# A slot list built from one-hot factors: token columns laid out in pairs, the 112-column factor held stationary

## The reference

```
topv, topi = lax.top_k(probs, K)                          # K = 2 experts for each token
mask = flat_i[None, :] == jnp.arange(E)[:, None]
pv, pp = lax.top_k(jnp.where(mask, flat_v[None, :], -1.0), capacity)
tok = jnp.where(pv > 0.0, pp // K, 0)
xin = x_flat[tok]                                         # 8 x 444 rows of 256
h = gelu(einsum('ecd,edh->ech', xin, w1) + b1)
out_e = (einsum('ech,eho->eco', h, w2) + b2) * w
out = zeros.at[tok.reshape(-1)].add(out_e)                # then a layer norm and the residual
```

## Time and profile before

| | |
|---|---|
| median of 3 runs | 497.82 us (497.4 to 695.03) |
| profiled execution | 497.69 us, its span 496.0 us |
| mean granted TensorE clock | 0.861 of 2.4 GHz |
| busy: PE, DVE, ACT, POOL | 376.4, 330.7, 210.0, 239.3 us |

### The profile page before, as it was taken

The page is one execution under the profiler, slowest core; times in us unless marked ns, Lnnn a source line. Parts: engine busy times, 40 slices in busy tenths (PEclk is TensorE's granted clock), DMA queues, the critical chain, the costliest instruction groups (busy, mean ns, idle before and its releaser), DMA issues.

```text
span 496.0 us, 7921 instructions
## 1 busy us (share of the span) xinstructions
PE 376.4 (76%) x2309; PEld 333.4 (67%) x2309; DVE 330.7 (67%) x863; ACT 210.0 (42%) x466; POOL 239.3 (48%) x399
## 2 busy tenths in 40 slices
PE   4585999999999998430136799999999999992000
PEld 1485999999999997330023599999999999991000
DVE  6463688777787866788881366667666676740692
ACT  4222445445445443272000256565656556532241
POOL 3254777777777755300002600835537274044395
PEclk9779899999999998755555699999999999997555
DMA  6423123323323201290002323656546475132833
GB/s 188 108 85 104 45 76 103 91 74 109 86 78 109 65 28 58 74 152 1 0 22 83 92 86 106 150 156 165 114 130 138 151 173 134 17 39 28 212 92 105
DMA packets 44676, 47.42 MB, mean 96 GB/s; under 512 B 11851, under 2 KB 36550, under 8 KB 44646
## 3 DMA queue, kind: packets, MB, share of 16 engines
q1 hardware_dynamic: 37940, 38.91, 28.0%
q0 software_dynamic: 5632, 7.36, 9.1%
q10 hardware_dynamic: 1074, 0.79, 0.6%
HBM read 32.38 MB, written 14.67 MB: 95 GB/s over the span
## 4 chain that ended last, share of the span: by engine, by line
PE 69%; DVE 12%; POOL 6%; DMA 4%; SPq 3%; issue 2%; ACT 1%; ACTq 0%; POOLq 0%; DVEq 0%
PE pz L796 16%; PE pall L809 16%; PE pall L703 9%; PE pall L672 8%; DVE wproj L1071 5%; PE pall L679 3%; SPq L423 3%; PE pall L769 2%; PE pall L713 2%; PE pz L659 2%; POOL stage L1354 2%; PE pall L720 1%; PE pall L821 1%; DMA stage<-in_x 1%; PE pall L692 1%
## 5 line engine op out<-in xcount | busy, mean ns | idle before, releaser
L1325 POOL DMA_INDIRECT y_rows<-rows,didx x32 | 50.7, 1585 | 95.2 <-ACT rows L606 87.9
L796 PE MATMUL pz<-halves 128*128 128x448 f32 x384 | 90.6, 373 | 2.1 <-DVE halves L1153 2.1
L809 PE MATMUL pall<-halves 128*128 128x448 f32 x384 | 89.9, 369 | 0.6 <-DVE halves L1148 0.6
L796 PEld LDWEIGHTS pz<-halves 128*128 128x128 f32 x384 | 73.7, 192 | 8.8 <-DVE halves L1153 2.5
L809 PEld LDWEIGHTS pall<-halves 128*128 128x128 f32 x384 | 70.9, 188 | 6.8 <-DVE halves L1148 1.0
L590 ACT ACTIVATE wproj<-pz,b1t 128x448 f32<-128x448 f32 x64 | 40.6, 635 | 73.8 <-PE pz L796 70.3
L1315 POOL DMA_INDIRECT rows<-x_rows,gidx x32 | 34.6, 1082 | 69.6 <-DVE gidx L1133 60.0
L703 PE MATMUL pall<-halves 128*112 128x256 f32 x396 | 55.1, 296 | 9.0 <-DVE halves L981 9.0
L1146 DVE CAST halves<-wproj 128x448 fp32r<-128x448 f32 x64 | 26.6, 416 | 50.0 <-ACT wproj L590 46.0
L703 PEld LDWEIGHTS pall<-halves 128*112 128x112 f32 x396 | 50.8, 186 | 9.9 <-DVE halves L981 7.4
L1223 POOL TENSOR_TENSOR rs<-rs,neghalf 112x1 f32<-112x1 f32 x88 | 50.1, 570 | 7.3
(11 more groups left out here) (211 smaller groups left out, 736.3 us busy)
## 6 DMA issues: line engine op xcount, KB each, us to landing
stage<-in_w SPq DMA_DIRECT2D x32, 512.0 KB, 4.2
stage<-in_x SPq DMA_DIRECT2D x64, 108.0 KB
x_rows<-x SPq DMA_DIRECT2D x22, 224.0 KB, 3.3
y_rows<-zero SPq DMA_DIRECT2D x22, 112.0 KB
stage<-y_rows SPq DMA_DIRECT2D x3, 448.0 KB, 5.4
out<-stage SPq DMA_DIRECT2D x7, 192.0 KB
scratch<-y_rows SPq DMA_DIRECT2D x2, 448.0 KB, 8.5
wproj<-in_w_proj ACTq DMA_DIRECT2D x1, 768.0 KB
```

What stands on the lines that cost most here:

```text
L796: m = nc.tensor.matmul(bank(k % 2)[:, 0:SLOTS], w[:, c, k * 128:(k + 1) * 128], xs[:, e % 2, c, :], start=(n == 0), stop=(n == 3 * EC - 1))
L809: m = nc.tensor.matmul(pall[:, 2 * (e % 2) + o, 0:SLOTS], w[:, k, o * 128:(o + 1) * 128], hs[:, k % 2, :], start=(k == 0 and n == 0), stop ...
L1325: pool.indirect_dma_start(y_rows, bass.IndirectOffsetOnAxis(ap=didx[:, k:k + 1], axis=0), y[:, e % 2, j, :], None, compute_op=ALU.add).the ...
```

## The change

The two factors get another layout, the matmul's operands change places, and the transposition behind it goes.

- `ohlo` is laid out as [22 pairs, 112 rows, 2] and `ohhi` and `ohval` as [22 pairs, 32 columns, 2]: the innermost two elements are the token columns 2i and 2i+1. Neighbouring columns of one q are then 2 elements, 4 bytes, apart.
- The tables hold each number twice in place of 44 times, and the comparisons read them again for each pair (`each_pair`), as they read `hi`, `lo` and `code` again for each column (`by_pair`). The number of elements that each DVE instruction computes stays the same: 1408, 1408, 2464 and 2464.
- Each of the 44 matmuls takes `ohlo` (112 columns) as the stationary operand and `ohval` (32 columns) as the moving one. The result is [112, 32], in the bank from which `gidx` was read before.
- The copy to `listT`, the transpose, and the two waits between them are gone.

```diff
-        ohlo = rows[:, 0:Q * P // 2].bitcast(bf16).rearrange("p (c q) -> p c q", q=Q)
-        ohhi = rows[:, Q * P // 2:Q * (P + COLS) // 2].bitcast(bf16).rearrange("p (c q) -> p c q", q=Q)
+        ohlo = rows[:, 0:Q * P // 2].bitcast(bf16).rearrange("p (q c k) -> p q c k", c=P, k=2)
+        ohhi = rows[:, Q * P // 2:Q * (P + COLS) // 2].bitcast(bf16).rearrange("p (q c k) -> p q c k", c=COLS, k=2)
-        ohval = sb("ohval", [P, COLS, Q], bf16)
+        ohval = sb("ohval", [P, Q // 2, COLS, 2], bf16)
-        lotab = sb("lotab", [P, P, Q], bf16)
-        hitab = sb("hitab", [P, COLS, Q], bf16)
-        listT = sb("listT", [COLS, P])
+        lotab = sb("lotab", [P, P, 2], bf16)
+        hitab = sb("hitab", [P, COLS, 2], bf16)
-        def over_q(a):
-            return rep(a.rearrange("p (a q) -> p a q", a=1), 1, COLS)
+        def by_pair(a, n):
+            return rep(a.rearrange("p (q a k) -> p q a k", a=1, k=2), 2, n)
+
+        def each_pair(tab, n):
+            return rep(tab.rearrange("p (a c) k -> p a c k", a=1), 1, n)
-            nc.scalar.copy(hitab[:, :, :], rep(iorow[:, 0:COLS].rearrange("p (c a) -> p c a", a=1), 2, Q)).then_inc(r_tab, 1)
-            nc.scalar.copy(lotab[:, :, :], rep(locen[:, :].rearrange("p (c a) -> p c a", a=1), 2, Q)).then_inc(r_tab, 1)
+            nc.scalar.copy(hitab[:, :, :], rep(iorow[:, 0:COLS].rearrange("p (c a) -> p c a", a=1), 2, 2)).then_inc(r_tab, 1)
+            nc.scalar.copy(lotab[:, :, :], rep(locen[:, :].rearrange("p (c a) -> p c a", a=1), 2, 2)).then_inc(r_tab, 1)
-                m = nc.tensor.matmul(bank(6)[0:COLS, 0:P], ohval[:, :, q], ohlo[:, :, q],
+                m = nc.tensor.matmul(bank(7)[0:P, 0:COLS], ohlo[:, q // 2, :, q % 2], ohval[:, q // 2, :, q % 2],
                                      start=(q == 0), stop=(q == Q - 1))
             m.then_inc(r_list, 1)
-            pe.wait_ge(r_list, 2)
-            nc.tensor.transpose(bank(7)[0:P, 0:COLS], listT[:, :], ident[0:COLS, 0:COLS]).then_inc(r_list, 1)
-            link(V_.tensor_tensor(ohhi, over_q(hi[:, :]), hitab[:, :, :], ALU.is_equal))
-            V_.tensor_tensor(ohval[:, :, :], ohhi, over_q(code[:, :]), ALU.mult).then_inc(r_val, 1)
+            link(V_.tensor_tensor(ohhi, by_pair(hi[:, :], COLS), each_pair(hitab[:, :, :], Q // 2), ALU.is_equal))
+            V_.tensor_tensor(ohval[:, :, :, :], ohhi, by_pair(code[:, :], COLS), ALU.mult).then_inc(r_val, 1)
             link(V_.scalar_tensor_tensor(lo[:, :], hib[:, :], -float(P), s12f, ALU.mult, ALU.add))
             for h in range(2):
-                qs = slice(h * Q // 2, (h + 1) * Q // 2)
-                V_.tensor_tensor(ohlo[:, :, qs], rep(lo[:, qs].rearrange("p (a q) -> p a q", a=1), 1, P),
-                                 lotab[:, :, qs], ALU.is_equal).then_inc(r_lo, 1)
+                qs = slice(h * Q // 4, (h + 1) * Q // 4)
+                V_.tensor_tensor(ohlo[:, qs, :, :], by_pair(lo[:, h * Q // 2:(h + 1) * Q // 2], P),
+                                 each_pair(lotab[:, :, :], Q // 4), ALU.is_equal).then_inc(r_lo, 1)
             dve.wait_ge(r_list, 1)
-            V_.tensor_copy(listT[:, :], bank(6)[0:COLS, 0:P]).then_inc(r_list, 1)
-            dve.wait_ge(r_list, 3)
-
             listed = bank(7)[0:P, 0:COLS].bitcast(u32)
```

## The result

The changed kernel takes 490.07 us in the median of 4 runs (489.28 to 490.32), the kernel before 497.61 (495.08 to 695.03): a ratio of 0.9846 with a 95% interval of 0.9824 to 0.9868. In a second comparison on one chip with three other kernels it was 489.28 against 497.41, 0.9825 (0.980 to 0.985). Forecast were 489.9 us and a range of 488.4 to 494.0. The 695.03 us is one slow run among the four of before, and the ratio leaves it out.

The account below looks back on a forecast made before the run. The prediction took the single file of routing work, with 44 list matmuls at 88 bytes between columns, as the bound: 497.69 - 7.95 (`gidx` earlier) + 0.1 (clock) = 489.8 us, stated as 489.9, range 488.4 to 494.0.

Parts of the forecast that it names:

- The spacing of the matmuls: List matmuls on TensorE: 0.094 us from start to start in place of 0.260, the price of a 112-column load.
- the rival that rested on the other reading, 188 ns a pair: List matmuls: the stationary operand is read at the rate of 4-byte data, 493.9 us; chance 0.10.
- the one with 260: List matmuls: any gap between columns costs what it does now, leaving the transposition's 0.65 us, 497.0 us; chance 0.04.
- The sum: List stage: matmuls at 0.094 us, copy and transpose gone; `gidx` moves from 268.10 to 260.15, 7.95 us.
- The list's length: The 44 list matmuls: first at 255.82 as now, last start 259.86, list done at 260.12.
- The comparisons: DVE's comparisons before the list keep their counts and times, 0.89 and 1.44 us.
- the slower rival: DVE comparisons: each row of two elements costs extra; at 5.2 ns a row, 509 us; chance 0.03.
- The collision with the weights: Gathers behind `gidx`: the first two meet the second expert's weights, the last does not; charged nothing, up to 1 us as bound.
- The margin to the splits: Before `gidx`: DVE's splits end at 259.42 and do not hold it; margin 0.7 us.
- The clock: TensorE at the feed-forward start: same cold start, no gain from the shorter list; 0.1 us added, bound 2.3 less or more.
- the 4 to 5 given as a sign: Feed-forward start: if the forecast is right, the clock rises 4 to 5 us behind the first L796.
- the case better than the sum: Loads shorter, `gidx` follows the splits at 259.45, clock rises 1 us or more earlier: below 487.9 us; chance 0.03.

Follow-up runs that it names:

- three other kernels: Changed kernel plus unread matmuls: 18 behind the list, 487.87 us; 20 more in front, 488.71; the same with index ahead of the w2 splits, 488.37.
- the runs on the pitch: Changed kernel with 1, 4, 11 or 22 token columns side by side instead of 2 (2, 8, 22, 44 bytes): 492.67, 490.20, 493.82, 494.20 us.
- the run with 2 bytes: Changed kernel with the columns of one token column side by side, no pairs, each row of the comparisons one token column: 492.67 us.
- The last run above: Changed kernel plus 18 unread matmuls behind the list and 20 in front, with the index ahead of the two w2 splits on DVE: 488.37 us, 0.9812.
- the repeat: The changed kernel itself run again, on one chip with three kernels given extra matmuls: 489.28 us, 0.9825 against before.
- the two profiles whose list began at 2.4 GHz: Changed kernel with unread matmuls on both sides of the list, 488.71 us, and the same with index ahead of the w2 splits, 488.37 us.

## Why the prediction was right, point by point

- **The spacing of the matmuls.** Predicted 0.094 us from the difference of two loads, measured 0.093. This is the term that carries the forecast, and the runs on the pitch bear it out: 112 close columns cost 112 cycles, in either place. The guess that a contiguous f32 load goes over its columns twice was not tested by itself, but the rival that rested on the other reading, 188 ns a pair, is refuted, and so is the one with 260.
- **Pitch, not operand.** The sum charged the load's 112 columns as it would have charged 112 moving ones. The run with the old operand order shows that this was sound at 4 bytes (0.093 us apart at 1.2 GHz in either place), and that the swap is the small part. At 88 bytes the two differ: 0.214 and 0.260.
- **The list's length.** Predicted 4.30 us from the first matmul's start to the end (255.82 to 260.12), measured 4.27; `gidx` 4.33 behind the start, measured 4.29. The step at `gidx` was 7.95, measured 7.99.
- **The comparisons.** Taken as unchanged, and unchanged. The Trainium skill (Vector Engine (DVE) Microarchitecture Reference, section 5.1) has two results a cycle for 16-bit operands with step one and an innermost count above one; the trace agrees at a count of 2 (0.89 us for 1408), and the run with 2 bytes shows the lost rate (1.63) once an operand is read at step 0. A cost for each row of two, the slower rival, is below what the trace resolves.
- **The collision with the weights.** It is there, as forecast, and hidden, as forecast. The first gathered block is transposed 3.63 us behind its issue (259.88 to 263.51) where it was 3.05, but the last lands 2.65 us behind its issue against 2.70. The last run above has a stronger collision: the second gather landed 4.52 us after its issue, still ahead of the last, and it cost 0.6 us through what had queued up behind it on TensorE, filling matmuls among it.
- **The margin to the splits.** 0.7 us predicted, 0.68 measured as DVE's wait.
- **The clock.** No rise inside the list and a cold start of the same kind: right. The rise itself came 3.5 us behind the first L796 in the first profile and 5.3 in the repeat, both outside the 4 to 5 given as a sign (and before it was 4.4; 4.7 was the end of the window that the prediction read). Mis-sized was the price of the cold start. Its bound of 2.3 us up or down took all of the half-clock stretch as time on the path; the runs show 1.1 to 1.7 in all, because ACT and DVE take 1.9 us behind the first 6 matmuls whatever the clock, and the next 6 have that time to run in. A rise 1 us earlier, on which the case better than the sum counted, is worth nothing by itself: after had it, and took the same 4.5 us to the second product as before. The range was a little wider below than it need have been.
- **The number.** That the time met 489.9 us to within 0.7 in both comparisons is in part luck. The 7.99 us of the list are the forecast's 7.95; the untouched start alone differed by 0.73 us between the two profiles, and the cold start varies by 0.6 from one execution to the next.

What stays open: what decides when the clock rises and falls around the list, and where between 8 and 22 bytes the large step lies. No run was made for either.

## What to carry to other kernels

When small matmuls run at several cycles a column, look at how many bytes lie between neighbouring columns of both operands before anything else: here 4 in place of 88 was worth 7.3 us, and at 4 bytes it mattered little which operand was stationary (at 88 bytes the stationary place was the cheaper one). Lay the data out so that the reader's columns are close and the writer's innermost row is still long enough for its own rate; two 16-bit elements were enough. And price a cold TensorE only over the matmuls that stand in the chain, not over the whole stretch at half clock.

## What the runs showed of the hardware

- TensorE counts as busy through 44 matmuls in all layouts, but of the eleven profiles whose list began at a granted 1.2 GHz only the one that streamed 112 close columns in each got 2.4 GHz inside the list. Being busy did not raise the clock by itself: not in 11.6 us at 88 bytes with 112 streamed columns, not in 9.2 at 88 bytes with 32, not in 4.3 at 4 bytes with 32.
- In the two profiles whose list began at 2.4 GHz, with 32 streamed columns behind loads of 112, the clock fell to 1.2 inside the list, after 16 and after ten matmuls. TensorE had stood idle for 3.1 and 1.7 us just before, so whether the idle time or the kind of matmul let it fall is not shown.
- 8 bytes between bf16 columns already cost about 12% (0.105 against 0.093 us), 22 bytes twice as much, and 44 and 88 bytes the same as each other.
- At 88 bytes a moving operand is dearer than a stationary one: 2.3 against 1.9 ns a column at 1.2 GHz.
